# Half of an out-projection moved into the scan phase, and the chunks of the second phase staged anew

## The chip, the cores and the metric

The kernel runs on one core of one Trainium2 chip. The metric is the device time of one execution in microseconds (us); before the change its median is 3416.74 us over three runs (3415.76 to 3419.22). Lower is better.

## The reference, cut to what matters

Three layers of a decoder on x of shape (2, 2048, 512): a selective-scan mixer, cross attention over a context of 77 keys with 16 heads, and a feed-forward part with a sine in it. Each is followed by a residual sum and a layer norm.

```
xz = x @ W_in + b_in                      # 512 -> 2048, halves x_proj and z
u = silu(x_proj); B, C = split(u @ W_xproj + b_xproj)
dt = softplus(u @ W_dt + b_dt)
h[t] = h[t-1] * exp(dt * A) + dt * u * B  # 16 states for each of 1024 channels
y = (sum over states of h * C + D * u) * silu(z)
x = layernorm(x + y @ W_out + b_out)                                  # x1
x = layernorm(x + softmax(mask(q k^T / sqrt(32))) v @ wo + b_o)       # x2
hidden = x @ W1 + b1                                                  # 512 -> 2048
q = hidden + gain * sin(theta + 0.1 * hidden)
x = layernorm(x + relu(q) @ W2 + b2)
```

Both batches make 4096 tokens. Products with large weights are done with operands split in a high and a low float16 half, in three matmuls each (`split_product`, lines 40 to 42).

## The kernel before

**Phase one, the scan** (`selective_scan_phase`). Tokens are columns. There are 8 chunks of 512 tokens, and in each 64 "pairs" of two states for 128 channels. For each pair PE spreads dt and dt*u over the partitions (`rep_dt`, L295; `rep_dtu`, L306), ACT takes the exponential in PSUM (`exps`, L526), DVE multiplies by B (`dbu`, L642) and runs two scans (`scans`, L655), ACT saves the last column (`save_carry`, L532), POOL multiplies by C (`weigh`, L722), and PE sums over states (`sums`, L318). PE, ACT and POOL also produce the projections of the next chunk within the pairs of the running one, at places that class `Plan` gives by hand. In the last chunk nothing is left to produce after place 28; keys and values of the cross attention are made at places 40, 42, 44 and 46 (`KV_AT`). y goes to DRAM, transposed, 128 channels at a time (`store_y`).

**Phase two, attention and feed-forward** (`attention_ffn_phase`). All engines meet at the end of phase one, and then walk over 16 chunks of 256 tokens (two tiles of 128). The order on each engine is written out by hand in `front_back(c, ...)`: the front of chunk c (out-projection, x1, attention, x2) and the back of chunk b = c-1 (feed-forward) are interleaved. Body 0 has a front only, body 16 a back only; bodies 2 to 14 are loops. What matters here:

- PE computes `out_projection` of chunk c (48 matmuls of 512 columns) at the start of the body, into the two PSUM banks `sps`. Then come the transposes of x2 and x1, `hidden` 0 to 7 (two of 16 columns of w1 each, into two PSUM buffers `fps`), `second` 0 to 7 (w2, into `nat`), the queries' projection, `scores`, `probs_t` (transposes of the probabilities), `attend` (times v) and at the end `natural(... w_o ...)`, again into `sps`.
- ACT: `hid_out` (four evacuations), `sine`, `relu`, `exps`, `probs_out`, `values_high`; its tables for square root, sine and exponential change four times in a chunk.
- DVE: residuals, layer norm (`statistics`, `normalize`), `fraction` (two instructions, both operands in SBUF), `mix` (two), `act_low`, `masked`, `row_maximum`, `less_maximum`, `softmax_b`.
- POOL: bias adds of 128x1024 (L1524) and the low half of y (`y_low`, L1533).

The body 0 also splits w1 and w2 in high and low, piece by piece.

## Time and profile before

| what | us |
|---|---|
| profiled execution, its own time | 3416.91 |
| its span | 3415.2 |
| last scan chunk (64 pairs), first dbu to last scan | 1738.2 to 1966.3 |
| last store of y issued; first load of phase two issued | 1971.9; 1974.4 |
| body 0: queries' projection; first scores | 2009.6 to 2016.9; 2018.0 |
| last w_o matmul of chunk 0, and of chunk 15 (start of its residual on DVE, less 0.2) | 2062.4; 3351.2 |
| x2's bias add on POOL, first and last (15 chunks between) | 2071.3; 3357.3 |
| a chunk in the loop (2585.32 to 2670.66) | 85.34 |
| from the last w_o matmul to x2 normalized (2661.78 to 2665.82) | 4.0 |
| PE, three pairs with 24 projection matmuls, one `sums` and one skip product (1751.6 to 1760.8) | 9.2 |
| busy over the span: PE, DVE, ACT, POOL | 86%, 80%, 59%, 52% |
| a load of 1024 KB of y_t, of 512 KB of x, issue to landing (median) | 7.5, 8.1 |
| `y_low` 128x2048, `y` to high 128x2048 | 4.07, 1.91 |
| keys of one batch, values of one batch, on PE | 4.5 to 6.2, 4.1 |

Read it so: the chunks of phase two take 85.9 us each on average ((3351.2 - 2062.4) / 15), and they are 1289 of the 3415 us. In rows of the timeline the first number is the start, the second the time from the first start to the last end of the merged instructions or their sum; a matmul's record is longer than its share of PE, so a block's price is the distance between the starts of two blocks.

### The profile page before, as it was taken

What the parts mean: (1) busy time and instruction counts of PE and PEld (TensorE: products, weight loads), DVE (VectorE), ACT (ScalarE), POOL (GpSimd) and SP (SyncE); (2) the same over time, 40 slices, a digit from 0 to 9 for tenths busy, and PEclk for the clock granted to TensorE, in tenths of its full rate; (3) what the DMA queues carried; (4) which work ended last, traced back from release to release, by engine and by line L of the source; (5) the groups of instructions that cost most, each with busy time, mean ns of one, the idle gap of its engine ahead of it and who ended that gap; (6) DMA issues with size and microseconds to landing.
All of it is one profiled execution on the core that took longest, in us unless ns stands there. A gap on an engine that the chain in (4) does not pass through costs nothing. (4 is left out here: it accounts for less than half of the span.)

```text
span 3415.2 us, 49521 instructions
## 1 busy us (share of the span) xinstructions
PE 2934.8 (86%) x18996; PEld 1318.5 (39%) x18996; DVE 2738.8 (80%) x3098; ACT 1999.3 (59%) x3570; POOL 1777.3 (52%) x893
## 2 busy tenths in 40 slices
PE   5888879889889888798897849999999999999997
PEld 2222222222222222222221236666666666666664
DVE  3999999999999999999999966666666666666664
ACT  4776776677667667766775444444444444444444
POOL 3797988978888879889788611111111111111100
PEclk8999999999999999999997769999999999999999
DMA  4111111111111111111113140000000000000000
GB/s 144 50 47 59 48 55 41 47 59 47 35 59 53 47 61 47 54 41 47 59 41 112 34 150 8 26 26 25 25 25 25 26 26 25 25 25 25 25 7 13
DMA packets 92547, 153.66 MB, mean 45 GB/s; under 512 B 12002, under 2 KB 29026, under 8 KB 91875
## 3 DMA queue, kind: packets, MB, share of 16 engines
q1 hardware_dynamic: 92386, 151.54, 14.0%
q8 instruction: 99, 1.62, 0.2%
q14 instruction: 62, 0.50, 0.1%
HBM read 92.79 MB, written 58.72 MB: 44 GB/s over the span
## 5 line engine op out<-in xcount | busy, mean ns | idle before, releaser
L722 POOL TENSOR_TENSOR h<-h,c_rep 128x1024 f32<-128x1024 f32 x512 | 1198.3, 2355 | 309.4 <-ACT carry L532 308.7
L655 DVE TENSOR_TENSOR_SCAN h<-r_ps,carry,h 128x512 f32<-128x512 f32 x768 | 942.8, 1272 | 7.2 <-ACT r_ps L526 6.5
L526 ACT ACTIVATE r_ps<-r_ps,decay 128x512 f32<-128x512 f32 x1024 | 632.0, 656 | 334.0 <-PE r_ps L295 333.3
L642 DVE TENSOR_TENSOR h<-u_ps,b_rep 128x1024 f32<-128x1024 f32 x512 | 618.7, 1208 | 44.3 <-PE u_ps L306 43.5
L1524 POOL TENSOR_TENSOR x<-x,rows 128x1024 f32<-128x1024 f32 x32 | 76.4, 2388 | 975.8 <-PE tr L961 975.8
L306 PE MATMUL u_ps<-dtu,spread 32*128 32x512 f16 x2048 | 326.6, 398 | 110.5 <-DVE h L642 109.4
L295 PE MATMUL r_ps<-dt,spread 32*128 32x512 f16 x2048 | 324.5, 396 | 75.5 <-DVE h L655 62.7
L318 PE MATMUL y_ps<-h,gather 128*32 128x512 f32 x2048 | 297.6, 650 | 55.6 <-POOL h L722 55.6
L655 DVE TENSOR_TENSOR_SCAN h<-r_ps,zero,h 128x512 f32<-128x512 f32 x256 | 313.9, 1269 | 6.9 <-ACT r_ps L526 6.7
L40 PE MATMUL nat<-region,act 128*128 128x512 f16 x512 | 206.8, 404 | 94.5 <-DVE act L1378 48.4
L40 PE MATMUL fps<-x,region 128*128 128x256 f16 x1024 | 280.9, 274 | 3.8 <-issue 2.4
L41 PE MATMUL fps<-x,region 128*128 128x256 f16 x1024 | 280.5, 274 | 0.0
L42 PE MATMUL fps<-x,region 128*128 128x256 f16 x1024 | 280.4, 274 | 0.0
L295 PEld LDWEIGHTS r_ps<-dt,spread 32*128 32x128 f16 x2048 | 58.5, 93 | 430.0 <-DVE h L655 244.0
L1154 ACT ACTIVATE units<-fps,turns 128x256 f32<-128x256 f32 x256 | 106.9, 468 | 191.7 <-PE fps L42 190.9
L40 PE MATMUL pj<-x_high,region 128*128 128x512 f16 x484 | 191.8, 396 | 31.7 <-ACT zs L467 12.6
L532 ACT ACTIVATE carry<-h 128x2 f32<-128x2 f32 x512 | 103.1, 201 | 189.9 <-DVE h L655 188.4
L40 PE MATMUL pj<-u_high,region 128*128 128x512 f16 x512 | 204.5, 399 | 4.9 <-ACT soft L499 3.7
L41 PE MATMUL nat<-region,act 128*128 128x512 f16 x512 | 205.0, 400 | 0.0
L42 PE MATMUL nat<-region,act 128*128 128x512 f16 x512 | 204.8, 400 | 0.0
L41 PE MATMUL pj<-u_low,region 128*128 128x512 f16 x512 | 203.0, 397 | 0.0
L42 PE MATMUL pj<-u_high,region 128*128 128x512 f16 x512 | 202.9, 396 | 0.0
(222 smaller groups left out, 5653.8 us busy)
## 6 DMA issues: line engine op xcount, KB each, us to landing
u_t_dram<-u SPq DMA_DIRECT2D x16, 1024.0 KB, 4.9
z_t_dram<-zs SPq DMA_DIRECT2D x32, 512.0 KB, 3.0
uz<-u_t_dram SPq DMA_DIRECT2D x64, 256.0 KB, 3.8
uz<-z_t_dram SPq DMA_DIRECT2D x64, 256.0 KB, 4.2
y_t_dram<-y SPq DMA_DIRECT2D x64, 256.0 KB, 2.4
y_t<-y_t_dram SPq DMA_DIRECT2D x15, 1024.0 KB, 7.5
x_in<-dram_x SPq DMA_DIRECT2D x16, 512.0 KB, 8.1
result<-x SPq DMA_DIRECT2D x16, 512.0 KB, 3.4
```

Of the source, the lines that this page charges most:

```text
L40: nc.tensor.matmul(out, w[0], x[0], start=start, stop=False)
L41: nc.tensor.matmul(out, w[0], x[1], start=False, stop=False)
L42: return nc.tensor.matmul(out, w[1], x[0], start=False, stop=stop)
L295: last = nc.tensor.matmul(r_ps[:, 2 * (pair % 2) + o, :], spread[32 * i:32 * i + 32, p // 2, :], dt16[32 * i:32 * i + 32, s, j, :], start= ...
L306: last = nc.tensor.matmul(u_ps[:, o, :], spread[32 * i:32 * i + 32, p // 2, :], dtu16[32 * i:32 * i + 32, s, j, :], start=(s == 0), stop=( ...
L318: last = nc.tensor.matmul(y_ps[32 * i:32 * i + 32, :], gather[:, q, :], h[:, g % H_GROUPS, i, :], start=(q == 0), stop=(q == 3))
L526: nc.scalar.activation(bank, bank, ACT.Exp, scale=decay[:, col:col + 1]).then_inc(s_da, 1)
L532: nc.scalar.activation(carry[:, j * NSTATE + 2 * p:j * NSTATE + 2 * p + 2], h[:, pair // 2 % H_GROUPS, o:o + 2, TS - 1], ACT.Copy).then_in ...
L642: nc.vector.tensor_tensor(h[:, g % H_GROUPS, o:o + 2, :], u_ps[:, :, :], b_rep[:, c % 2:c % 2 + 1, :].broadcast_to([P, 2, TS]), ALU.mult). ...
L655: nc.vector.tensor_tensor_scan(row, r_ps[:, 2 * (pair % 2) + o, :], row, start, ALU.mult, ALU.add)\
L722: nc.gpsimd.tensor_tensor(rows, rows, c_rep[:, c % 2:c % 2 + 1, :].broadcast_to([P, 2, TS]), ALU.mult)\
L1154: nc.scalar.activation(arg[:, n % 3, i, :], fps[:, n % 2, i, :], ACT.Identity, bias=turns[:, f:f + 1], scale=UNSCALE * 0.1 / TWO_PI)
```

## The change

1. `out_projection` leaves the chunk. For chunks 0 to 7 (16 tiles of 128 tokens) it runs in the last scan chunk, at pairs 28 to 59, half a tile (12 matmuls) in each pair; w_out is split there at places 18 to 28, y tiles are read back from DRAM, and the product goes to a DRAM tensor `o`. For chunks 8 to 15 it runs in bodies 0 (three chunks), and 1 to 5 (one each), behind the queries' projection, a tile at a time; its result goes to `o` too.
2. Keys and values move from places 40, 42, 44, 46 to 60, 61, 62, 63.
3. x1 is x + o + b_out, added on POOL (two adds of 128x1024), in the body before; its layer norm is in the middle of the body before.
4. `second` 6 and 7 of a chunk move into the next body, in front of and behind x1's transposes; there are 18 bodies now, and the final layer norm is one body later. x1 and x2 have two buffers each. x1's transposes and the queries use `sps`, not `tr`.
5. Within a chunk `hidden` 0 and 1 stand in front of the queries' projection.
6. `scores` interleaves two lanes (two groups of 32 rows), where it took one lane after the other.
7. POOL's x2 bias add waits for half of the scores.

Phase one (the constants and the pieces on PE and POOL):

```
-KV_AT = (40, 42, 44, 46)
+KV_AT = (60, 61, 62, 63)
+OUT_TILES = 16
+W_OUT_AT, OUT_AT = 18, 28
...
+            def out_piece(i, part):
+                if part == 0:
+                    pe.wait_ge(s_oe, i) if i else pe.wait_ge(s_ev, NC * PIECES)
+                pe.wait_ge(s_yl, 2 * i + part + 1)
+                for k in range(4 * part, 4 * part + 4):
+                    tokens = slice(k % 4 * P, k % 4 * P + P)
+                    last = split_product(nc, pj[:, :], [y16[s][:, i % 4, part, tokens] for s in range(2)],
+                                         [w_out[s][:, k, :] for s in range(2)], k == 0, k == NJ - 1)
+                if part == 1:
+                    last.then_inc(s_op, 1)
...
+            def w_out_low(k):
+                pool.wait_ge(s_wos, k // 2 + 1)
+                nc.gpsimd.tensor_tensor(w_out[1][:, k, :], w_out_raw[:, k, :], w_out[0][:, k, :], ALU.subtract)\
+                    .then_inc(s_wol, 1)
+
+            def y_low(i, r):
+                g = i % 4
+                pool.wait_ge(s_yh, i + 1)
+                nc.gpsimd.tensor_tensor(y16[1][:, g, r, :], w_out_raw[:, 2 * g + r, :], y16[0][:, g, r, :], ALU.subtract)\
+                    .then_inc(s_yl, 1)
```

Phase two, the order on PE:

```
+    def body(c, par, batch, front, back, late, ops, more):
+        b, d = c - 1, c - 2
+        if late:
+            second(d, 6)
+        if front:
+            x1_transposed(c, par, back)
+        if late:
+            second(d, 7)
+        if back:
+            x2_transposed(c, par)
+        if back:
+            hidden(b, 0)
+            hidden(b, 1)
+        if front:
+            queries(c)
+        for m in ops:
+            out_projection(c, m, 0)
+            out_projection(c, m, 1)
+        if back:
+            hidden(b, 2)
+        if front:
+            scores(c, 0, batch, (0, 1), ops)
+        if front:
+            scores(c, 0, batch, (2, 3), ops)
         if back:
             hidden(b, 3)
             second(b, 0)
         if front:
+            scores(c, 1, batch, (0, 1), ops)
+        if back:
+            hidden(b, 4)
             second(b, 1)
         if front:
+            scores(c, 1, batch, (2, 3), ops)
+        if back:
+            hidden(b, 5)
             second(b, 2)
+            hidden(b, 6)
             second(b, 3)
+        if front:
+            probs_t(c, 0, (0, 1))
+        if back:
             hidden(b, 7)
         if front:
             probs_t(c, 0, (2, 3))
         if back:
+            second(b, 4, (0,))
         if front:
             attend(c, 0, batch)
             probs_t(c, 1, (0, 1))
         if back:
+            second(b, 4, (1,))
         if front:
             probs_t(c, 1, (2, 3))
         if back:
+            second(b, 5, (0,))
         if front:
             attend(c, 1, batch)
         if back:
+            second(b, 5, (1,))
+        if front:
+            attention_out(c)
```

The order on ACT, its later part:

```
+    def body(c, par, batch, front, back, late, ops, more):
...
+            relu(b, 2)
             sine(b, 3)
+            hid_out(b, 4)
             relu(b, 3)
             sine(b, 4)
+        if front and not back:
+            weights_high(6)
+        if front:
+            exps(c, 0)
+        if back:
             hid_out(b, 5)
             relu(b, 4)
         if front:
+            exps(c, 1)
+        if more:
+            deviation("x1", 0, c + 2)
+        if back:
+            sine(b, 5)
             hid_out(b, 6)
+            relu(b, 5)
             sine(b, 6)
+        if front and not back:
+            weights_high(7)
+        if front:
+            probs_out(c, 0, (0, 1))
+        if back:
             hid_out(b, 7)
+        if front:
+            probs_out(c, 0, (2, 3))
+        if back:
             relu(b, 6)
             sine(b, 7)
         if front:
             values_high(c, 0)
             probs_out(c, 1, (0, 1, 2, 3))
```

The order on DVE, from the first `fraction` on:

```
+    def body(c, par, batch, front, back, late, ops, more):
+        b, d = c - 1, c - 2
...
         if back:
             fraction(b, 0)
             fraction(b, 1)
             mix(b, 0)
+        if front:
+            masked(c, 0, (0, 1))
+            masked(c, 0, (2, 3))
+        if back:
             fraction(b, 2)
             act_low(b, 0)
+            mix(b, 1)
+        if front:
+            row_maximum(c, 0)
+            masked(c, 1, (0, 1))
+        if back:
+            act_low(b, 1)
+            fraction(b, 3)
+            mix(b, 2)
+        if front:
+            masked(c, 1, (2, 3))
+            less_maximum(c, 0)
+        if back:
+            act_low(b, 2)
+            mix(b, 3)
+        if front:
+            row_maximum(c, 1)
+        if back:
+            fraction(b, 4)
+            act_low(b, 3)
+        if front:
+            less_maximum(c, 1)
+        if back:
+            mix(b, 4)
+        if front:
+            probabilities(c, 0)
+        if back:
+            act_low(b, 4)
+            fraction(b, 5)
+        if more:
+            statistics("x1", 0, c + 1, x1[:, 1 - par, :, :])
+        if front:
+            probabilities(c, 1)
+        if more:
+            normalize("x1", 0, c + 1, x1[:, 1 - par, :, :])
+        if back:
+            mix(b, 5)
             fraction(b, 6)
+            act_low(b, 5)
             mix(b, 6)
             fraction(b, 7)
             act_low(b, 6)
...
```

The order on POOL:

```
+    def body(c, par, batch, front, back, late, ops, more):
+        for m in ops:
+            for t in range(NT):
+                y_low(m * NT + t, t)
+        if front:
+            x1_bias(c, par)
+        if back:
+            pool.wait_ge(s_scp, b_scores(c, front))
+            x2_bias(c - 1, 1 - par)
+        if more:
+            x1_sum(c + 1, 1 - par)
+    def b_scores(c, front):
+        return c * 8 + 4 if front else CHUNKS * 8
```

`softmax_b` is now named `probabilities`. `x1_sum` is two adds of 128x1024 (o and b_out, then x), `x1_bias` and `x2_bias` one each.

## Rows read from the trace of the kernel before

**Rows 1.** Windows of the last scan chunk: us, busy of each engine, granted clock, DMA.
```profile
1780.00:1820.00 40.00, 34.77 (x208) 10.01 (x207) 39.89 (x36) 29.06 (x55) 37.03 (x21) 0.99 0.11 34
1820.00:1860.00 40.00, 30.53 (x160) 5.66 (x160) 39.59 (x36) 20.49 (x43) 36.91 (x21) 0.71 0.53 186
```

**Rows 2.** Timeline of PE in one chunk: start, us, engine, line, operands, idle before.
```profile
2491.09 0.38 PE L40 MATMUL sps<-w_out,y 128*128 128x512 f16 x1
...
2498.86 1.04 PE L961 MATMUL tr<-ident,x 128*128 128x128 f32 x8
...
2502.53 0.28 PE L40 MATMUL fps<-x,region 128*128 128x256 f16 x1
...
2511.03 1.09 PE L961 MATMUL tr<-ident,x 128*128 128x128 f32 x8 [0.46 <-DVE x L1356]
...
2517.69 0.38 PE L40 MATMUL nat<-region,act 128*128 128x512 f16 x1 [2.95 <-issue]
...
2520.28 0.27 PE L40 MATMUL tr<-xa,w_q 128*128 128x256 f16 x1
...
2528.20 1.62 PE L992 MATMUL sps<-k_t,q_t 32*128 32x77 f32 x16
2529.76 0.28 PE L40 MATMUL fps<-x,region 128*128 128x256 f16 x1
```

**Rows 3.** Timeline of DVE in one chunk, from the last scores on.
```profile
2627.51 0.99 DVE L1394 TENSOR_TENSOR pr<-sps,cap 128x308 f32<-128x308 f32 x2 [2.09 <-PE sps L992]
2628.53 1.44 DVE L1400 TENSOR_REDUCE smax<-pr 128x16 f32<-128x1232 f32 x1
2629.89 0.42 DVE L1362 TENSOR_SCALAR units<-units 128x512 f32<-128x512 f32 x1
...
2630.94 0.68 DVE L1378 SCALAR_TENSOR_TENSOR act<-units,act 128x512 f16<-128x512 f32 x1
2631.55 1.44 DVE L1404 TENSOR_TENSOR pr<-pr,smax 128x1232 f32<-128x1232 f32 x1
2632.90 1.43 DVE L1411 TENSOR_REDUCE ssum<-pr 128x16 f32<-128x1232 f32 x1
...
2636.01 0.42 DVE L1362 TENSOR_SCALAR units<-units 128x512 f32<-128x512 f32 x1
...
2640.18 1.66 DVE L1373 SCALAR_TENSOR_TENSOR units<-units,gain 128x256 f32<-128x256 f32 x4
```

**Rows 4.** Timeline of ACT in the same chunk.
```profile
2633.33 0.84 ACT L1154 ACTIVATE units<-fps,turns 128x256 f32<-128x256 f32 x2 [2.23 <-PE fps L42]
...
2634.78 1.24 ACT L1174 ACTIVATE pr<-pr 128x1232 f32<-128x1232 f32 x1
2636.04 1.28 ACT L1164 ACT_TABLE_LOAD   x1
```

**Rows 5.** Timeline of body 0: POOL and DVE beside each other.
```profile
2003.21 2.99 POOL L1524 TENSOR_TENSOR x<-x,rows 128x1024 f32<-128x1024 f32 x1 [17.92 <-PE tr L961]
...
2003.92 4.44 DVE L1293 SCALAR_TENSOR_TENSOR region<-act,region 128x2048 f16<-128x2048 f32 x1
...
2021.65 4.36 POOL L1533 TENSOR_TENSOR y<-y_t,y 128x2048 f16<-128x2048 f32 x1 [15.45 <-ACT y L1127]
2022.02 4.09 DVE L1383 TENSOR_SCALAR cap<-mask_i 128x154 f32<-128x154 int32 x1
```

**Rows 6.** Source line L1383 on DVE: durations in ns, min/median/max.
```profile
L1383 DVE TENSOR_SCALAR cap<-mask_i x16: 233/235/4094, 2022.0 to 3302.4; 128x154 f32<-128x154 int32 x16
```

**Rows 7.** Timeline of PE in body 0, the first matmuls after an idle stretch.
```profile
2009.64 0.37 PE L40 MATMUL tr<-xa,w_q 128*128 128x256 f16 x1 [6.51 <-DVE xa L1299]
...
2010.23 0.42 PE L40 MATMUL tr<-xa,w_q 128*128 128x256 f16 x1
2010.44 0.42 PE L41 MATMUL tr<-xa,w_q 128*128 128x256 f16 x1
...
2013.99 0.27 PE L40 MATMUL tr<-xa,w_q 128*128 128x256 f16 x1
```

More of the change, by code:

```diff
@@ L981, in hidden, with second, scores @@
                     last.then_inc(s_hp, 1)
-            def scores(c, t, batch, lanes):
+            def second(b, n, tiles=range(NT)):
+                if n == 0:
+                    pe.wait_ge(s_wlo, W2_SPLIT)
+                    pe.wait_ge(s_rw2, b * NT)
+                pe.wait_ge(s_actl, b * NU + n + 1)
+                for t in tiles:
+                    last = natural(nat[:, t, :], act16, w_2, NF, t, 2 * n, 2 * n + 2)
+                    if n == NU - 1:
+                        last.then_inc(s_w2, 1)
+            def scores(c, t, batch, lanes, ops):
                 for lane in lanes:
@@ L1078, in front_back @@
                     hidden(b, 5)
-                if front:
-                    scores(c, 1, batch, (2, 3))
-                if back:
+                    second(b, 2)
+                    hidden(b, 6)
                     second(b, 3)
-                    hidden(b, 6)
-                    second(b, 4)
-                    hidden(b, 7)
                 if front:
@@ L1266, in front_back @@
                 if back:
-                    relu(b, 7)
-                if not back:
-                    weights_high(10)
+                    relu(b, 6)
+                    sine(b, 7)
                 if front:
@@ L1272, in front_back @@
                     probs_out(c, 1, (0, 1, 2, 3))
+                if back:
+                    relu(b, 7)
+                if front:
                     values_high(c, 1)
-                if not back:
-                    weights_high(11)
-                if back and not front:
-                    deviation("w2", 2, b)
-            all_chunks(act, front_back)
+                if front and not back:
+                    weights_high(8)
+                    weights_high(9)
+            all_chunks(act, body)
         @block.vector
@@ L1443, in front_back @@
-                    normalize("outproj", 0, c, x1)
-                if not back:
-                    weights_low(4)
-                    weights_low(5)
+                    mask(c)
+                if late:
+                    normalize("w2", 2, d, x2[:, par, :, :])
+                if front and not back:
+                    for n in range(2, 6):
+                        weights_low(n)
                 if back:
@@ L1478, in front_back @@
                 if front:
-                    masked(c, 1, (2, 3))
-                    row_maximum(c, 1)
+                    probabilities(c, 0)
                 if back:
+                    act_low(b, 4)
                     fraction(b, 5)
-                    act_low(b, 4)
+                if front and not back:
+                    weights_low(6)
+                if more:
+                    statistics("x1", 0, c + 1, x1[:, 1 - par, :, :])
                 if front:
-                    less_maximum(c, 1)
@@ L1509, in front_back @@
                 if back:
[L1510 to L1511 removed]
+                    act_low(b, 7)
+                if front and not back:
+                    weights_low(8)
+                    weights_low(9)
                 if front:
[L1513 to L1517 removed]
@@ L1519, in _ @@
-            all_chunks(dve, front_back)
+                    for t in range(NT):
+                        residual_wo(c, par, t)
+            all_chunks(dve, body)
         @block.gpsimd
         def _(pool):
-            def add_bias(x, row, done):
-                nc.gpsimd.tensor_tensor(x[:, :, :], x[:, :, :], rows[:, row:row + 1, :].broadcast_to([P, NT, D]), ALU.add)\
-                    .then_inc(done, 1)
-            def bias_x_in(c):
-                pool.wait_ge(s_xin, (c + 1) * 16)
-                add_bias(x_in, 0, s_xb["xin"])
@@ new lines, in _, with body @@
+            pool.wait_ge(s_rows, 3 * 16)
+            x1_sum(0, 0)
+            def body(c, par, batch, front, back, late, ops, more):
+                for m in ops:
+                    for t in range(NT):
+                        y_low(m * NT + t, t)
+                if front:
+                    x1_bias(c, par)
+                if back:
+                    pool.wait_ge(s_scp, b_scores(c, front))
+                    x2_bias(c - 1, 1 - par)
+                if more:
+                    x1_sum(c + 1, 1 - par)
```

685 lines of the change are left out of this document (368 added, 317 removed).

## The prediction, on record before the result

> **What bounds the kernel now.** I read the windows first, then PE's timeline over one chunk of phase two, then DVE, ACT and POOL beside it. In the last scan chunk DVE is busy for 39.9 of 40 us while PE has 34.8 and, once production is over, 30.5 at a clock of 0.71 [rows 1]: DVE sets the pace, at 228.3 / 64 = 3.57 us a pair (its back-to-back distance is 3.48), and POOL with 37 of 40 is close behind. In phase two PE sets it. A chunk of 85.3 us has few idle places on PE, such as the 2.95 us ahead of `second` 0 [rows 2]. Distances between starts price PE's blocks: a matmul of 512 columns 0.215 us (12 in 2.59), one of 256 columns 0.11, two lanes of scores 1.56, the out-projection 7.77 for its first 36 matmuls and 10.35 for all 48 [rows 2]. All blocks of a chunk sum to 75.9 us, 9.4 of 85.3 are idle.
>
> **The chunk without the out-projection.** PE's work falls to 65.5, and to about 62.4 if two lanes of scores take 0.8 instead of 1.56. That would be 23 us less a chunk, but only if PE is never kept waiting, so I walk through the new orders with the distances of rows 3 and 4: `fraction` 1.05, `mix` 0.8, `act_low` 0.6, `masked` of two lanes 0.95, `row_maximum` and `less_maximum` 1.35 each, `probabilities` 3.1 (2632.90 to 2636.01) [rows 3]; `hid_out` 1.45, exponential 1.25, table load 1.28, sine and relu 0.55 [rows 4]. Zero is the last w_o matmul of the chunk before.
> - x2 is normalized at 4.0, as now. PE meanwhile has `second` 6, x1's transposes, `second` 7 and reaches x2's transposes at 6.05; high half on ACT to 8.2, low half on DVE to 9.5, `hidden` 0 starts at 9.7 (2.8 us idle). `hidden` 1 ends at 14.9, the queries at 20.2, `hidden` 2 at 22.8.
> - Scores of lanes 0 and 1 to 23.6; `masked` to 24.8; lanes 2 and 3 to 25.7 (1.3 us idle, since they wait for both banks); `masked` to 26.8. `fraction` 2, `act_low` 0: done 28.5, just when `hidden` 3 ends on PE. Then `second` 0, scores, `hidden` 4, `second` 1, scores: 38.0.
> - From 38.2 DVE has no gap but 0.4: `masked` 0.95, `less_maximum`, `act_low` 2, `mix` 3, `row_maximum`, `fraction` 4, `act_low` 3, `less_maximum`, `mix` 4, `probabilities` 0, `act_low` 4, `fraction` 5, x1's statistics 1.6, `probabilities` 1, x1's normalize 1.1, `mix` 5, `fraction` 6: 22.3 us, to 60.5. ACT's `sine` 6 waits for that, and `probs_out` of the first quarters stands behind it in ACT's order. PE is through with `hidden` 7 at 54.2 and waits in `probs_t(c, 0, (2, 3))` until 61.1: 7 us, with `second` 4 and 5 queued behind.
> - Behind it 15.1 us of work (transposes 1.8, `second` 4 and 5 5.2, `attend` 2.0, w_o 5.2, and 0.9 for the second half of the quarters) and small waits: **77.0 us**.
>
> So even without disturbance 14 to 15 us of the 23 come back as waits: PE's list was shortened where it was not the only limit.
>
> **POOL in the chunk.** New is where POOL's adds stand. When DVE or POOL works with operands in SBUF, one is held by the other: `mask`'s instruction of 0.23 us took 4.09 beside `y_low` [rows 5, 6], and it ended with it. Of two DVE instructions in a row, the waiting POOL add came between (its record is 2.99 instead of 2.36, and the second DVE instruction 4.44 instead of 2.29) [rows 5]. Now POOL's x2 bias add is released by half of the scores, at 25.8, and two more adds (o with b_out, x with o) stand behind it at once: 7.1 us. `fraction` 2 at 26.8 is held to 28.2, its second instruction by the second add to 31.0, `act_low` 0 by the third to 34.0. `second` 0 starts at 34.7, not 28.6: +6.1, and everything behind it moves along. Bounds: 0, if the adds let DVE through, and 7.1.
>
> The Trainium skill ("SBUF — State Buffer", Who interferes with whom) says that a DVE instruction with two SBUF inputs, or in a two-port mode, and a GpSimd instruction exclude each other for a whole instruction, and that issue order decides. By issue order alone, with DVE's next instruction issued ahead of POOL's next add, `act_low` 0 would slip through earlier, the delay would be about 3, and the sum below some 45 us smaller; the alternation seen in this trace speaks for 6.1.
>
> **The clock.** After 6.5 us of idle PE ran at half speed (0.21 us a matmul of 256 columns, against 0.11) from 2009.6 to 2013.9 [rows 7]; that loses 2.1 us. The new chunk has two such gaps, 6.4 us ahead of `second` 0 and 7 us ahead of `probs_t`. I count the first fully, 2.1, and 0.4 for the second, whose slow matmuls run beside ACT's `hid_out` 7 and `probs_out`. Bounds: 0 and 5. A chunk: 77.0 + 6.1 + 2.5 = **85.6**, against 85.9 on average now.
>
> **Scores in pairs.** Two lanes are 1.56 us now, one behind the other [rows 2]; no row has them interleaved. `rep_dt` and `rep_dtu`, which do interleave groups of 32 rows, put four matmuls of 512 columns into 0.43 us. I take 0.8; the bounds are 0.4 and 1.6, so a chunk is at most 3 longer.
>
> The Trainium skill ("TensorEngine Tiling (Array Packing)", Key Properties) has tiles of 32 rows work in parallel in weight load and matmul, which gives the 0.8; by the row of the sequential lanes alone the sum would be 45 us larger.
>
> **Chunks with out-projection.** Bodies 1 to 5 have 48 more matmuls behind the queries: 5 x 10.35 = +51.7. y's halves are ready in time there (its loads have a whole body, POOL's two halves of 2.05 lie ahead of the place that hurts), and nothing behind them had slack to give back.
>
> **Body 0.** It has three chunks' worth. PE's part is 31.0 instead of 10.35, +20.7, and that is the lower bound. But `y_t` holds one tile now, so each tile goes load (5, an estimate between nothing for its half size and 8.1 for as many KB of x), high half 1.0, low half 2.05, about 8.6 with hand-overs, where its matmuls take 5.2. Queries end near 2007 in old times, 10 us earlier, since x1 no longer waits for a product; six tiles end near 2060; scores start there and not at 2018: +42. The 4.09 + 2.7 us that the mask lost go away, x1's norm of the next chunk and one more weight piece come in: +40 to +44. I take **+42**, bounds 21 and 55.
>
> **The scan's last chunk.** Out-projection puts 12 matmuls, 2.58 us, on PE in each of 32 pairs. Three pairs with 24 such matmuls took 9.2 us; less these and one skip product that leaves 0.66 a pair for the two spreads and 1.0 for `sums` of every second pair; with the skip product of every eighth, 2.58 + 0.66 + 0.5 + 0.13 = 3.87 a pair against DVE's 3.5: PE becomes the bound, 32 x 0.35 = +11. Its clock is full then. POOL gets 8 pieces of w_out of 1.15 in places 20 to 27, where it was at 37 of 40 us [rows 1]: +5, and half a tile of y in each later pair (2.36 + 1.15 = 3.5, just inside). Keys and values, 17 us on PE, lay beside DVE's work at places 40 to 46; at 60 to 63 only four pairs are left to hide them, and `sums` of the last pairs, the last store and the end of the phase wait behind them: +9. Sum **+25**, bounds 5 (all hidden but a few waits) and 45.
>
> **The end.** Bodies 16 and 17: `hidden` 0 starts 9.7 instead of 8.4 after the last w_o, but PE has run before it; the last `second`s and the norm are the same. 0.
>
> **The sum**: 25 + 42 + 51.7 + 15 x (85.6 - 85.9) = 114. From the profiled execution, 3416.9 (0.2 from the median of the runs), to **3530**. Solved for the chunk, the change pays only under 85.9 - 118.7 / 15 = 78.0 us.
>
> **The rivals.**
> 1. *The chunk really gets shorter (faster).* If POOL's adds do not get in between, the chunk is 77.0, or less where an engine starts earlier than I walked; with PE's 11 us in the scan and 25 in body 0 the sum is 11 + 25 + 51.7 - 133.5 = -46: 3371. It decides from 78.0 us a chunk down. For it: PE loses 13.5 us of work a chunk. Against it: the 7 us wait for DVE's list does not depend on POOL. Chance 0.26.
> 2. *POOL costs half.* A chunk of 80 and the rest as forecast: 118.7 - 88.5 = +30, 3447. The alternation speaks against it. 0.14.
> 3. *The clock goes down for longer.* PE's share of the chunk falls from 89% to 73%, and in the last scan chunk, where it is like that, the clock was 0.71 [rows 1]. Four gaps at 2.1 and the scores at 1.5: a chunk of about 91.5, sum 118.7 + 84 = +203: 3620. Against it: single gaps of 3 us left no trace in most chunks. 0.10.
>
> **How the numbers follow.** Forecast 0.50, its own range 3485 to 3585. The range 3370 to 3590 takes in the first two rivals but for half of the first, and leaves out the third. What can be told from no change is 0.2%, 7 us. Faster 0.25, same 0.02, slower 0.73: the sums of the cases with a point from each side for the middle.
>
> **What would show it.** Right: PE in a chunk of the loop idle in front of `nat` (`second` 0) for about 6 us with `act_low` 0 as releaser, and about 7 in front of `probs_t`; `fraction` and `act_low` with records of 2 to 3 us beside L1524's successors; chunks of 83 to 88; the last scan chunk near 250; the first w_o of body 0 some 65 us later than before. Wrong: no long DVE records, a chunk below 78; or a body 0 as long as before.

## The result, and the profile after

The changed kernel takes 3570.09 us (median of four runs, 3568.44 to 3570.57) where the kernel before, in runs beside it, took 3416.76. The ratio is 1.0447, with a 95% interval of 1.0429 to 1.0465: 4.5% slower. The prediction was 3530.

The profiled executions (spans 3415.2 and 3568.9) divide at three events that both have: SP's first load of phase two, the last residual of x2 in chunk 0, and the one in chunk 15.

| stage | before | after | difference | predicted |
|---|---|---|---|---|
| up to the first load of phase two | 1974.4 | 2003.7 | +29.3 | +25 |
| body 0, to its last x2 residual | 88.2 | 131.6 | +43.4 | +42 |
| 15 chunks, to the last x2 residual of chunk 15 | 1288.7 | 1374.3 | +85.6 | +47.2 |
| the end | 63.8 | 59.3 | -4.5 | 0 |

A chunk of the loop is 88.7 us ((3456.61 - 2658.52) / 9, from the start of x2's bias add on POOL), one with an out-projection 99.0 (2372.63 to 2471.63). The scan's last chunk and body 0 have the size of the forecast. The chunk of the loop is 3.1 us longer than the forecast's 85.6; over the fifteen chunks that makes 38.4 and not 46, since the last of them, with little behind it, takes only 80.6.

The windows of the last scan chunk, as [rows 1], and two more behind them (columns as there):
```profile
1780.00:1820.00 40.00, 35.48 (x212) 9.84 (x204) 39.03 (x35) 30.90 (x55) 36.05 (x21) 0.96 0.07 27
1820.00:1860.00 40.00, 26.51 (x136) 7.12 (x136) 28.75 (x26) 23.30 (x45) 38.92 (x27) 0.70 0.41 129
1860.00:1900.00 40.00, 40.00 (x252) 13.69 (x252) 36.06 (x32) 21.93 (x42) 36.47 (x24) 1.00 0.61 189
1900.00:1940.00 40.00, 40.00 (x256) 13.79 (x249) 37.36 (x34) 22.93 (x43) 36.05 (x21) 1.00 0.32 99
```
From 1820 to 1860 DVE is busy for 28.8 us where it had 39.6 [rows 1], and POOL is full with 38.9. From 1860 on PE is busy for all 40 us at a granted clock of 1.00, and DVE no longer is: PE is the bound now.

PE's timeline over one chunk of the loop, as [rows 2] (start, us, engine, line, operands, idle before). Zero of the prediction's walk is 3074.05 here.
```profile
3083.64 0.27 PE L40 MATMUL fps<-x,region 128*128 128x256 f16 x1 [2.50 <-issue]
...
3090.54 0.27 PE L40 MATMUL sps<-xa,w_q 128*128 128x256 f16 x1
...
3098.50 1.12 PE L1166 MATMUL sps<-k_t,q_t 32*128 32x77 f32 x16
...
3100.65 1.55 PE L1166 MATMUL sps<-k_t,q_t 32*128 32x77 f32 x16 [1.04 <-DVE pr L1542]
...
3110.58 0.38 PE L40 MATMUL nat<-region,act 128*128 128x512 f16 x1 [4.47 <-DVE act L1527]
...
3114.95 1.12 PE L1166 MATMUL sps<-k_t,q_t 32*128 32x77 f32 x16
...
3135.05 1.09 PE L1180 MATMUL sps<-ident,pr 128*77 128x128 f32 x8 [1.74 <-DVE pr L1562]
...
3145.52 1.96 PE L1180 MATMUL sps<-ident,pr 128*77 128x128 f32 x8 [6.76 <-ACT p_t L1347]
```
The walk had `hidden` 0 at 9.7 (here 9.6), `second` 0 at 34.7 (36.5), and 7 us of idle time ahead of the second `probs_t` (6.76). Of the 1.8 us by which `second` 0 is later, 1.7 are `hidden` 0 and 1, which take 6.90 us and not 5.24. In phase two the waits of the `probs_t` for ACT's `p_t` sum to 103.8 us, the largest sum that PE has there; those of the `second`s for `act_low` sum to 71.7.

DVE and POOL in the same chunk, from the second pair of scores on; these rows answer to [rows 3] and [rows 5]:
```profile
3102.22 0.86 DVE L1542 TENSOR_TENSOR pr<-sps,cap 128x308 f32<-128x308 f32 x2 [1.62 <-PE sps L1166]
3102.31 2.35 POOL L1709 TENSOR_TENSOR x<-x,rows 128x1024 f32<-128x1024 f32 x1 [21.99 <-PE sps L1166]
3103.01 1.94 DVE L1512 TENSOR_SCALAR units<-units 128x512 f32<-128x512 f32 x1
3104.61 2.53 POOL L1698 TENSOR_TENSOR o_in<-o_in,rows 128x1024 f32<-128x1024 f32 x1
3104.98 2.71 DVE L1515 TENSOR_TENSOR units<-units 128x512 f32<-128x512 f32 x1
3107.22 2.66 POOL L1701 TENSOR_TENSOR x<-x,o_in 128x1024 f32<-128x1024 f32 x1
3107.61 2.82 DVE L1527 SCALAR_TENSOR_TENSOR act<-units,act 128x512 f16<-128x512 f32 x1
3110.36 0.87 DVE L1522 SCALAR_TENSOR_TENSOR units<-units,gain 128x256 f32<-128x256 f32 x2
```
POOL's three adds and DVE's `fraction` 2 and `act_low` 0 take turns, one instruction each. Three DVE instructions of 0.42, 0.69 and 0.68 us have records of 1.94, 2.71 and 2.82, and `act_low` 0 ends where PE's wait ends.

ACT in that chunk, as [rows 4], ahead of the second wait:
```profile
3134.80 1.28 ACT L1281 ACT_TABLE_LOAD   x1
3138.22 0.30 ACT L1281 ACTIVATE std<-mv,eps 128x2 f32<-128x2 f32 x1 [2.13 <-DVE mv L1499]
3138.53 1.28 ACT L1330 ACT_TABLE_LOAD   x1
...
3143.20 0.63 ACT L1336 ACTIVATE act<-units 128x512 f16<-128x512 f32 x1 [1.29 <-DVE units L1522]
3144.27 0.63 ACT L1330 ACTIVATE units<-units 128x512 f32<-128x512 f32 x1 [0.43 <-DVE units L1515]
3144.80 1.06 ACT L1347 ACTIVATE p_t<-sps 77x512 f32<-77x512 f32 x2
```
`probs_out` (L1347) has had its input since 3135.98 and starts at 3144.80, behind x1's square root, `sine` 5, `hid_out` 6, `relu` 5 and `sine` 6 in ACT's list.

Body 0, out-projection on PE (answers to [rows 7]; each row opens one tile, the tile at 2048 opens without a wait):
```profile
2040.69 0.61 PE L40 MATMUL sps<-w_out,y 128*128 128x512 f16 x1 [4.07 <-POOL y L1713]
...
2060.85 0.61 PE L40 MATMUL sps<-w_out,y 128*128 128x512 f16 x1 [6.79 <-POOL y L1713]
...
2068.71 0.39 PE L40 MATMUL sps<-w_out,y 128*128 128x512 f16 x1 [1.21 <-POOL y L1713]
...
2080.86 0.61 PE L40 MATMUL sps<-w_out,y 128*128 128x512 f16 x1 [6.79 <-POOL y L1713]
...
2088.12 0.39 PE L40 MATMUL sps<-w_out,y 128*128 128x512 f16 x1 [0.37 <-POOL y L1713]
...
2094.25 1.12 PE L1166 MATMUL sps<-k_t,q_t 32*128 32x77 f32 x16 [0.78 <-ACT o_out L1313]
```
The six tiles take 53.6 us, to the first scores. The mask's first instruction, 4.09 us before, is short there now; the longest of its 16 records is 2.07 (answers to [rows 6]):
```profile
L1532 DVE TENSOR_SCALAR cap<-mask_i x16: 206/224/2066, 2029.5 to 3439.7; 128x154 f32<-128x154 int32 x16
```

### The profile page after: what moved, and what is told of

It reads as the page before. It is cut to its first block and busy times, and to the rows that moved or that the text cites. A ratio compares the mean times of both kernels' runs of the same rounds, so it can differ in the third digit from the quotient of the medians.

```text
span 3568.9 us, 48928 instructions
## 1 busy us (share of the span) xinstructions
PE 2930.3 (82%) x18996; PEld 1309.3 (37%) x18996; DVE 2764.7 (77%) x3063; ACT 2038.5 (57%) x3638; POOL 1842.7 (52%) x950
## 5 line engine op out<-in xcount | busy, mean ns | idle before, releaser
L345 PE MATMUL u_ps<-dtu,spread 32*128 32x512 f16 x2048 | 319.4, 390 | 103.3 <-DVE h L731 102.7
L334 PE MATMUL r_ps<-dt,spread 32*128 32x512 f16 x2048 | 315.7, 388 | 57.2 <-DVE h L744 44.7
L357 PE MATMUL y_ps<-h,gather 128*32 128x512 f32 x2048 | 287.6, 630 | 57.5 <-POOL h L811 57.5
L40 PE MATMUL fps<-x,region 128*128 128x256 f16 x1024 | 294.7, 288 | 39.6 <-issue 31.7
L41 PE MATMUL fps<-x,region 128*128 128x256 f16 x1024 | 294.4, 288 | 0.0
L42 PE MATMUL fps<-x,region 128*128 128x256 f16 x1024 | 294.0, 287 | 0.0
L40 PE MATMUL nat<-region,act 128*128 128x512 f16 x512 | 211.1, 412 | 71.7 <-DVE act L1527 71.7
L1713 POOL TENSOR_TENSOR y<-y_t,y 128x1024 f16<-128x1024 f32 x16 | 36.3, 2270 | 411.5 <-ACT y L1307 411.5
L40 PE MATMUL pj<-x_high,region 128*128 128x512 f16 x484 | 192.0, 397 | 31.8 <-ACT zs L519 12.7
L41 PE MATMUL nat<-region,act 128*128 128x512 f16 x512 | 210.6, 411 | 0.0
L42 PE MATMUL nat<-region,act 128*128 128x512 f16 x512 | 208.7, 408 | 0.0
L40 PE MATMUL pj<-u_high,region 128*128 128x512 f16 x512 | 204.6, 400 | 4.9 <-ACT soft L551 3.8
```

The lines of the kernel that those rows point to most:

```text
L40: nc.tensor.matmul(out, w[0], x[0], start=start, stop=False)
L41: nc.tensor.matmul(out, w[0], x[1], start=False, stop=False)
L42: return nc.tensor.matmul(out, w[1], x[0], start=False, stop=stop)
L334: last = nc.tensor.matmul(r_ps[:, 2 * (pair % 2) + o, :], spread[32 * i:32 * i + 32, p // 2, :], dt16[32 * i:32 * i + 32, s, j, :], start= ...
L345: last = nc.tensor.matmul(u_ps[:, o, :], spread[32 * i:32 * i + 32, p // 2, :], dtu16[32 * i:32 * i + 32, s, j, :], start=(s == 0), stop=( ...
L357: last = nc.tensor.matmul(y_ps[32 * i:32 * i + 32, :], gather[:, q, :], h[:, g % H_GROUPS, i, :], start=(q == 0), stop=(q == 3))
```

## The experiments

Twelve kernels. Ratios are against runs of the kernel before on the same chip (medians 3419 to 3422), so the changed kernel, at 1.0447, is to be read beside them. "Loop chunk" is the mean of nine, measured as above; "out chunk" is the mean of the last three or four with an out-projection.

| run | us | ratio, 95% interval | first load of phase two | loop chunk | out chunk |
|---|---|---|---|---|---|
| changed kernel | 3570.1 | 1.0447, 1.0429 to 1.0465 | 2003.7 | 88.7 | 99.0 |
| a1_adds_early | 3476.2 | 1.0163, 1.0146 to 1.0180 | 2001.5 | 82.3 | 92.2 |
| a2_queries_first | 3512.3 | 1.0274, 1.0256 to 1.0292 | 2002.5 | 85.3 | 94.8 |
| a3_filler | 3554.9 | 1.0403, 1.0385 to 1.0420 | 2002.7 | 86.9 | 99.2 |
| a4_tiny_low | 3563.5 | 1.0427, 1.0410 to 1.0445 | 1998.3 | 88.7 | 98.9 |
| a5_act_order | 3535.1 | 1.0333, 1.0307 to 1.0359 | 2001.7 | 85.3 | 99.0 |
| a6_three | 3392.1 | 0.9928, 0.9912 to 0.9945 | 2001.9 | 77.1 | 85.3 |
| a7_two_of_three | 3559.2 | 1.0409, 1.0391 to 1.0426 | 1994.7 | 88.7 | 99.0 |
| a8_kv_quarter | 3570.6 | 1.0441, 1.0424 to 1.0459 | 2003.4 | 88.7 | 99.0 |
| a9_two_y | 3557.8 | 1.0406, 1.0388 to 1.0423 | 2005.1 | 88.7 | 99.0 |
| a10_more_act | 3380.0 | 0.9888, 0.9871 to 0.9904 | 2002.8 | 75.5 | 85.1 |
| a11_best | 3366.1 | 0.9839, 0.9826 to 0.9853 | 2002.4 | 75.8 | 85.1 |
| b1_lanes | 3407.1 | 0.9964, 0.9953 to 0.9976 | 1974.9 | | |

**POOL's adds (a1_adds_early).**
```
                 if back:
-                    pool.wait_ge(s_scp, b_scores(c, front))
                     x2_bias(c - 1, 1 - par)
```


> Changed kernel (3570), but POOL's x2 bias add no longer waits for half of the scores; it is released by x2's transposes, with the two adds for the next x1 behind it. Theory (the adds hold DVE's fraction 2 and act_low 0, and with them PE's second 0): the three adds now lie beside hidden 0 and 1, where DVE has little to do; in a plain chunk the idle time ahead of second 0 falls from 5.8 us to about 0 or 1, the chunk from 88.5 to about 81 to 83, total 3450 to 3490. Rival (the hold is covered by the later wait ahead of probs_t, so moving it only moves the wait): the gap ahead of second 0 goes, the one ahead of probs_t grows from 6.8 to 12, total 3550 to 3575. Rival 2 (the adds do as much harm where they stand now, delaying x2's low half): total 3560 to 3600.

Measured: 3476.2, a loop chunk 6.4 us shorter and an out chunk 6.8. The theory holds, the rivals do not: the wait ahead of `probs_t` stayed at 6.76. The three adds now lie here, in a timeline of DVE and POOL:
```profile
2928.86 2.34 POOL L1709 TENSOR_TENSOR x<-x,rows 128x1024 f32<-128x1024 f32 x1 [1.12 <-PE tr L1096]
2929.95 1.23 DVE L1471 TENSOR_TENSOR x<-tr,x 128x1024 f16<-128x1024 f32 x1 [1.04 <-ACT x L1293]
...
2931.15 2.35 POOL L1698 TENSOR_TENSOR o_in<-o_in,rows 128x1024 f32<-128x1024 f32 x1
...
2933.58 2.35 POOL L1701 TENSOR_TENSOR x<-x,o_in 128x1024 f32<-128x1024 f32 x1
2933.64 2.39 DVE L1534 TENSOR_SCALAR cap<-cap 128x154 f32<-128x154 f32 x1
```
x2's low half, which reads PSUM (L1471), runs at its usual 1.23 beside the first add. The mask's second instruction is held from 0.24 to 2.39, where nobody waits for it. The same adds now stand beside work with slack. The gain has two parts: `second` 0 comes 4.7 us earlier, and it runs at full speed (2.69 us for 4.37).

**Part 5 undone (a2_queries_first).**
```
+                if front:
+                    queries(c)
                 if back:
                     hidden(b, 0)
                     hidden(b, 1)
-                if front:
-                    queries(c)
```
(and the same on ACT.)

> Changed kernel (3570) with part 5 undone: the queries' projection stands in front of hidden 0 and 1 again, on PE, and its evacuation in front of theirs on ACT. Theory A (queries fill the 2.5 us of idle time ahead of hidden 0 and hidden runs at full clock): -3 to -4 us a chunk, total 3510 to 3525. Theory B (what decides is DVE's list from masked on: scores come 5 us earlier but fraction 0 to 2 come 5 us later, so second 0 waits as before): total 3555 to 3590.

Measured: 3512.3, a loop chunk 3.4 us shorter, an out chunk 4.2. Theory A. In the changed kernel `hidden` 0 comes 2.5 us after x2's transposes, since it needs their low half; the queries need only x1's, which has been there, and fill that time. The block of `hidden` 0 and 1, 6.90 us in the chunk of the changed kernel shown above (3083.64 to 3090.54), runs at full clock here: `hidden` 0 to 2 take 7.96, 2.65 each. `second` 0 still waits 5.67 us for `act_low` 0, as theory B had it, but starts 32.5 us after `second` 6 and not 36.5.

**The clock (a3_filler).**
```
                     hidden(b, 3)
+                    for k in range(16):
+                        mm(tr[:, 0:2, :].rearrange(...), w_1[:, 0, 0, 0:P], w_1[:, 0, k % KD, 0:512], ...)
                     second(b, 0)
```


> Changed kernel (3570) with 16 more matmuls of 512 columns into a bank that nobody reads then, between hidden 3 and second 0: about 3.4 us of work, put into the 5.8 us in which PE waits for act_low 0. Theory (after this gap second 0 runs at half clock, 4.4 us for 2.6): second 0 takes 2.6 to 3.0, a chunk of the loop -1 to -2 us, total 3545 to 3560. Rival (the slow matmuls lie beside DVE's work, which sets the next step anyway): no change within 5 us. Rival 2 (the filler delays second 0): slower, 3575 or more.

Measured: 3554.9, 1.8 us less a loop chunk. `second` 0 in the changed kernel, and with the filler in front of it (PE's timeline, both):
```profile
3110.58 0.38 PE L40 MATMUL nat<-region,act 128*128 128x512 f16 x1 [4.47 <-DVE act L1527]
...
3111.45 0.63 PE L41 MATMUL nat<-region,act 128*128 128x512 f16 x1
3111.88 0.63 PE L42 MATMUL nat<-region,act 128*128 128x512 f16 x1
...
3114.44 0.58 PE L42 MATMUL nat<-region,act 128*128 128x512 f16 x1
```
```profile
3005.92 3.62 PE L1227 MATMUL tr<-region 128*128 128x512 f16 x16
3010.59 0.38 PE L40 MATMUL nat<-region,act 128*128 128x512 f16 x1 [1.05 <-DVE act L1530]
...
3011.45 0.38 PE L41 MATMUL nat<-region,act 128*128 128x512 f16 x1
...
3012.96 0.38 PE L42 MATMUL nat<-region,act 128*128 128x512 f16 x1
```
The distance of two matmuls is 0.43 us in the one (1.2 GHz) and 0.215 in the other (2.4 GHz); the block takes 4.37 and 2.68. So the work that is late pays the clock on top of the wait. The loop chunks alternate between 85.4 and 88.5 with the filler, and so do two prices. In the chunk shown `hidden` 0 and 1 took 6.91 us, PE waited 1.05 us behind the filler, and `second` 0 took 2.68. In the chunk before it `hidden` 0 and 1 took 5.23, PE reached the filler earlier and then waited 2.24 us, and `second` 0 had 4.37 again. What makes `hidden` 0 and 1 differ, behind the same gap of 2.5 us, stays open.

**The scan: POOL's pieces (a4_tiny_low), PE's matmuls (a7_two_of_three), keys and values (a8_kv_quarter).**
```
-  nc.gpsimd.tensor_tensor(w_out[1][:, k, :], w_out_raw[:, k, :], w_out[0][:, k, :], ALU.subtract)
+  nc.gpsimd.tensor_tensor(w_out[1][:, k, 0:8], w_out_raw[:, k, 0:8], w_out[0][:, k, 0:8], ALU.subtract)
```


> Changed kernel (3570), with the low half of w_out in the scan phase computed for 8 of 512 columns only; this leaves most of that subtraction out. It takes 8 x about 1.1 us from POOL in places 20 to 27 of the last scan chunk. Theory (POOL's backlog of these pieces delays DVE, 11 us of idle time there): first load of phase two 9 to 13 us earlier than in the changed kernel (2003.7), total 3557 to 3561. Rival (PE's 3.75 us a pair behind it would have been the bound anyway, the backlog is absorbed): 0 to 3 us, total 3567 to 3570.


```
-  last = split_product(nc, pj[:, :], [y16[s]... for s in range(2)], [w_out[s][:, k, :] for s in range(2)], ...)
+  nc.tensor.matmul(pj[:, :], y16[0]..., w_out[0][:, k, :], ...)
+  last = nc.tensor.matmul(pj[:, :], y16[1]..., w_out[0][:, k, :], ...)
```


> Changed kernel (3570) with two of the three float16 products in the out-projection of the scan phase; the product with w_out's low half is left out there: 8 matmuls a pair, not 12, 0.86 us less on PE in each of 32 pairs. Theory (PE, at 3.75 us a pair, is the bound in places 32 to 59, DVE would go on at 3.5 to 3.57): first load of phase two 6 to 9 us earlier, total 3561 to 3564. Rival (POOL with 3.5 us a pair is the bound there as well): 0 to 3 us.


```
-  for k in range(KD):
-      last = nc.tensor.matmul(pj..., wk[:, k, ...], ctx_t[:, k, b, :], ...)
+  last = nc.tensor.matmul(pj..., wk[:, 0, ...], ctx_t[:, 0, b, :], ...)
```
(keys; the values' loop takes one k likewise.)

> Changed kernel (3570) with a quarter of the products for keys and values (the sum over 128 of 512 rows; three quarters are left out): PE's 17 us at places 60 to 63 become 4 to 5. Theory (only four pairs are left to hide them, and the last sums and the last store wait behind them): first load of phase two 8 to 13 us earlier, total 3557 to 3562. Rival (what ends the phase is DVE's last scans and the gate, or the loads for keys and values): 0 to 3 us.

The start of the last scan chunk differs from run to run by some us with the same code ahead of it (1745.84 to 1752.37), so the three are compared by its length, from the store of y that ends the chunk before to the last store. In the changed kernel these are (SP's timeline):
```profile
1748.09 0.32 SPq L228 DMA_DIRECT2D y_t_dram<-y  x1
...
1836.35 0.32 SPq L228 DMA_DIRECT2D y_t_dram<-y  x1
...
1877.23 0.32 SPq L228 DMA_DIRECT2D y_t_dram<-y  x1
...
1970.24 0.32 SPq L228 DMA_DIRECT2D y_t_dram<-y  x1
...
2001.26 0.33 SPq L228 DMA_DIRECT2D y_t_dram<-y  x1
```
| length of the last scan chunk | us |
|---|---|
| before (1745.89 to 1971.93) | 226.0 |
| changed | 253.2 |
| a4_tiny_low | 249.4 |
| a7_two_of_three | 243.2 |
| a8_kv_quarter | 248.5 |

With a third of the out-projection's matmuls gone eight pairs take 28.45 us again, not 31.0: PE is the bound there, for 10 us in all. POOL's pieces of w_out are 3.8 us, keys and values 4.7 for three quarters of their products. a8_kv_quarter missed its expectation of 8 to 13: its first load of phase two is 0.4 us earlier and its total did not move. In the profiled execution its scan chunk began 4.3 us later, so the 4.7 are read from the stage alone, from one execution each. a4_tiny_low missed its expectation of 9 to 13 as well: most of the idle time there lies ahead of the first half tile of the out-projection, whose matmuls wait for POOL's `y_low` behind POOL's other work and then run at half clock. Most of that wait stayed, 3.49 us where the changed kernel has 5.38 (PE):
```profile
1851.51 0.59 PE L40 MATMUL pj<-region,u_high 128*128 128x512 f16 x1 [5.38 <-POOL u_low L837]
```
They stand in PE's order ahead of the next pair's spreads, and DVE waits 6.96 us for these, its longest wait while the pairs run (5.88 in a4_tiny_low).

**ACT's order (a5_act_order).**
```
+                if front and back:
+                    probs_out(c, 0, (0, 1))
                 if more:
                     deviation("x1", 0, c + 2)
                 if back:
                     sine(b, 5)
                     hid_out(b, 6)
+                if front and back:
+                    probs_out(c, 0, (2, 3))
                 if back:
                     relu(b, 5)
                     sine(b, 6)
```


> Changed kernel (3570) with another order on ACT alone: the evacuation of the first two quarters of the probabilities (probs_out) stands ahead of x1's square root and sine 5, and that of the last two behind hid_out 6, not behind sine 6. Theory (the 6.8 us of PE's idle time ahead of the second probs_t comes of ACT's list, where probs_out stands behind sine 6, and DVE's list behind that has slack): the gap falls to 0 or 1, a chunk of the loop from 88.5 to 82 to 84, total 3470 to 3500. Rival (DVE's list is the bound there: the wait moves to second 5, which needs act_low 5 behind mix 5): 1 to 3 us a chunk, total 3520 to 3555.

Measured: 3535.1, loop chunk -3.4, out chunk 0. The theory's expectation was missed; the total lies in the range of the rival, but PE does not wait at `second` 5 as the rival had it. The 6.76 us are gone, and 1.98 and 2.99 come back ahead of `attend` and the last `probs_t`, both of them waits for `p_t` in ACT's list. The other 1.7 are speed: `hidden` 0 and 1 take 5.24 us in nine of ten loop chunks where they took 6.90. In an out chunk it is the other way round, 6.90 for 5.24, and that gives the 1.8 us of saved waits back.

**The three together (a6_three)**, a1, a2 and a5 in one kernel.

> Changed kernel with three edits: POOL's x2 bias add not held until half of the scores, queries in front of hidden 0 and 1, and the ACT order of the run a5_act_order. Measured alone, the first two take 6.4 and 3.2 us off a chunk of the loop (88.5). Theory (the three gaps are separate places on PE's path): chunk 72 to 75, total 3570 - 94 - 58 - 70 to 90 = 3330 to 3350, faster than the kernel before (3417 to 3420). Rival (DVE's work of some 60 us a chunk becomes the bound between masked and mix 5): chunk 77 to 79, total 3395 to 3430.

Measured: 3392.1 and 77.1 a loop chunk. Singly the three took 94, 58 and 35 us, 187 in sum; together 178. So the three gaps are separate. The total was over its expectation because a5 had been expected to bring twice what it did. The chunk of 77.1 is in the range that the rival had, and the total is 3 us under it, but its reason, DVE as the bound, is not what the rows show: DVE is busy for 67% of the loop, and of PE's 7.5 us of waits in a chunk 4.0 are for ACT's `p_t` and 3.6 for DVE.

**What is left on ACT (a10_more_act).**
```
                 if more:
                     deviation("x1", 0, c + 2)
+                if front and back:
+                    probs_out(c, 0, (2, 3))
                 if back:
                     sine(b, 5)
                     hid_out(b, 6)
...
+                if front:
+                    values_high(c, 0)
+                    probs_out(c, 1, (0, 1))
                 if back:
                     hid_out(b, 7)
```


> The kernel a6_three (3392) with two more moves on ACT: probs_out of the last two quarters of tile 0 ahead of sine 5, and values_high 0 and probs_out of tile 1's first quarters ahead of hid_out 7. Theory (PE's idle times of 1.98 us ahead of the first attend and 2.98 us ahead of the last probs_t come of ACT's order): chunk from 76.9 to 72 or 73, total 3315 to 3335. Rival (hid_out 7 and sine 6 come late, so the wait moves to second 5 or to the next body's second 7): 0 to 1 us a chunk, total 3375 to 3395.

Measured: 3380.0, in the range of the rival, with 1.6 us less a loop chunk. In the timeline of a6_three PE had these waits; in a10_more_act the first is gone and the second became 2.41, but one of 0.7 to 2.3 us now stands ahead of the second `attend`:
```profile
2925.76 1.08 PE L1189 MATMUL tr<-p_t,v 77*32 77x128 f32 x32 [1.98 <-ACT p_t L1347]
...
2932.15 1.78 PE L1180 MATMUL sps<-ident,pr 128*77 128x128 f32 x8 [2.98 <-ACT p_t L1347]
```
So the waits only moved: they sum to 67.7 us over nine loop chunks of a6_three and to 71.7 in a10_more_act. What fell is the time at half speed, from 2.9 to 1.8 us a chunk (counted as in the next section), with a mean granted clock of 0.94 and 0.96. That is 1.1 of the 1.6 us; the expectation's reason, less idle time, is not what the rows show.

**Body 0 (a9_two_y).**
```
+        def y_place(i):
+            if i < OPS_FIRST * NT and i % 2:
+                return x2[:, 1, :, :]..., s_yt[1], i // 2 + 1
...
+                    for i in range(NT * len(ops)):
+                        out_evacuated(i, i % 2)
+                        if i + 2 < NT * len(ops):
+                            y_high(i + 2, i % 2)
```


> Changed kernel (3570) with a second buffer for y tiles in body 0 (x2's second half, free there), and on ACT each tile's high half directly behind the evacuation of the tile two before. Theory (body 0's six tiles take a chain of load, high half, low half and 4 to 7 us of idle time on PE for every second tile, 53 us in all from the first matmul, where PE's work is 6 x 5.2 = 31): the first scores of body 0 start 17 to 22 us earlier against the first out-projection, total 3548 to 3554. Rival (body 0 is held by DVE's splitting of w1 and w2 and their loads, so that the wait only moves): 0 to 8 us.

Measured: 3557.8. The six tiles take 39.7 us, not 53.6, from 2041.69 to the first scores at 2081.34. The mechanism is shown, the size was over-expected: one wait of 4.46 us remains, for a y tile whose load lands only at 2065.07.

**Lanes of scores in pairs, in the kernel before (b1_lanes).**
```
-                    for i in range(HU):
-                        last = mm(sps[:, unit % 2, ...], q_t[rows_of, i, ...], k_t[rows_of, batch, i, :], ...)
-                    last.then_inc(s_scp, 1)
+                for i in range(HU):
+                    for lane in lanes:
+                        last = mm(sps[:, lane % 2, ...], q_t[rows_of, i, ...], k_t[rows_of, batch, i, :], ...)
```


> The kernel before (3416.8) with part 6 alone: the scores of two lanes interleaved, 32 matmuls alternating between two groups of 32 rows. Theory (four pairs of lanes a chunk, 1.05 instead of 1.56 us each, all on PE's path): -2 us a chunk, total 3380 to 3395. Rival (scores lie ahead of waits for DVE, so PE gains nothing): total 3412 to 3417. If interleaving brought what I had taken for the forecast (0.8): 3370.

Measured: 3407.1, 0.36% under the kernel before, some 12 us and not 30. Two lanes take 1.05 us, not 1.56. A loop chunk is as long as before (85.3 against 85.4 us). In one chunk read block by block the 2.0 us saved are gone again: `second` 0, behind the same idle time as before, took 3.79 us for 2.59, the queries' projection behind it 5.71 for 5.24, and the wait ahead of `second` 4 grew from 3.13 to 3.51. `second` 0 took 3.79 us or more in 14 of 15 chunks here, 3.80 or more in 4 of 15 before. The two windows around that `second` 0, first of b1_lanes, then of before:
```profile
2599.00:2604.00 5.00, 4.28 (x15) 1.83 (x16) 4.94 (x10) 4.33 (x9) 0.00 (x0) 0.71 0.00 0
```
```profile
2602.00:2607.00 5.00, 3.96 (x25) 2.44 (x26) 4.94 (x9) 4.66 (x10) 0.00 (x0) 1.00 0.00 0
```
The clock in them is 0.71 and 1.00, with an idle time of 2.95 and 2.96 us ahead of the block.

**The best of these (a11_best)** is a10_more_act with body 0 of a9_two_y.

> The kernel a10_more_act (3380) with the y tiles and the ACT order of a9_two_y in body 0. Measured in the changed kernel, these took 13.9 us off body 0's out-projection (53.56 to 39.65). Theory (body 0 and the chunks are separate terms of the sum): 3364 to 3368, 1.6% under the kernel before. Rival (with a shorter body 0, DVE's splitting of w1 and w2 comes late for the first chunks): 3372 to 3380.

Measured: 3366.1, as the sum of the terms had it, and 1.6% faster than the kernel before. So the change as a whole pays once its orders are put right. How much of this is the moved out-projection is not shown: 0.4% is what the scores in pairs gave alone, and no run puts the new order of ACT into the kernel before.

## Why the prediction was right or wrong

The sign and the places of the waits were right, 40 of 153 us were missing, and 38 of these lie in the chunk. There the cost of the clock was put far too low, and part of the agreement in the other terms is luck.

- *The scan's last chunk, +25.* It is 27.1 us longer; the other 2.2 lay ahead of it and are run-to-run. PE as the bound, 3.87 us a pair: 31.00 / 8 = 3.875 measured, and a7_two_of_three takes 10.0 back where 11 were counted. Keys and values, +9: the last interval between stores grew from 22.7 to 31.0, +8.3, but that holds out-projection too: a7_two_of_three takes 2.0 off it and a8_kv_quarter 4.8, so about 6 are keys and values, an estimate. POOL's backlog, +5: the pieces of w_out are 3.8, but the two intervals to 1877.23 are 14.7 us longer, because the first half tile of y waits in the same backlog and then runs at half clock. That wait was not in the forecast. It was offset by a gain that was not in it either: in the places 40 and on, keys and values had cost the kernel before 3.4 us (its three intervals from 1860.52 to 1949.26 are 88.7 us, three of 28.45 are 85.3; that keys and values are the reason is read from their place, no run shows it). That the stage came out near +25 is in part luck. The forecast's 228.3 us for the last scan chunk is 228.1 by its own events; nothing hangs on it.
- *Body 0, +42:* +43.4. The chain of 8.6 us a tile was right on average (53.6 / 6 = 8.9), and a9_two_y shows that it is the chain and not PE.
- *Five out-projections, 10.35 each:* the block takes 10.36. The difference of the chunks, 99.0 - 88.7 = 10.3, hides two terms that cancel: in an out chunk `hidden` 0 and 1 take 5.24 us for 6.90, but 0.98 of idle time stand ahead of the block and 5.64, not 4.47, ahead of `second` 0. In a6_three the difference is 8.2.
- *The chunk without disturbance, 77.0:* the gaps stand where the walk put them, and a6_three, without the hold and with shorter gaps at `hidden` 0 and at the second `probs_t`, comes to 77.1. The two numbers are not the same sum, and their agreement is luck: the walk had 14.6 us of idle time in a chunk (77.0 - 62.4), a6_three has 7.5 by its records and pays 2.9 of clock, which the walk did not. One part of the walk was added up wrongly: the steps listed from 38.2 on sum to 21.7 us with the gap of 0.4, not 22.3.
- *POOL's hold, +6.1:* a1_adds_early gives 6.4 a loop chunk, and in one of these chunks `second` 0 starts 31.8 us after `second` 6, where it was 36.5 (-4.7), and takes 2.69, not 4.37 (-1.7). So the hold itself was smaller than forecast, and the clock behind it was part of its price. Alternation, instruction by instruction, is what the rows show. The Trainium skill ("SBUF — State Buffer", Who interferes with whom) states an exclusive lock, and the trace agrees (0.69 us became 2.71 beside adds of 2.53 and 2.66). By issue order alone, its other statement, the forecast had estimated a delay of about 3, and a1_adds_early shows 4.7.
- *The clock, +2.5:* this is the step that failed in size. Counting in PE's timeline the matmuls of `hidden` and `second` that start at about twice the full-speed distance from the one before them, a loop chunk of the changed kernel loses 5.5 us, 2.9 in `hidden` and 2.6 in `second`. The kernel before loses 1.9, nearly all in `second`. The transposes behind the 6.76 us wait take 1.76 for 0.88. The forecast counted `second` 0 fully (1.8 to 2.6 measured) and nothing for `hidden` 0 and 1, which in nine of ten loop chunks took 6.6 to 6.9 us for 5.24, behind a gap of only 2.5. "Single gaps of 3 us left no trace in most chunks" holds for `second` 0 of the kernel before, 2.59 us behind 2.96 in 11 of 15 chunks. It does not hold for its `second` 4, which took 3.99 to 4.28 us in all 15, for the same 12 matmuls (kernel before, PE):
```profile
2603.04 0.38 PE L40 MATMUL nat<-region,act 128*128 128x512 f16 x1 [2.96 <-issue]
...
2642.51 0.61 PE L40 MATMUL nat<-region,act 128*128 128x512 f16 x1 [3.13 <-DVE act L1378]
```
- *Scores, 0.8 for two lanes:* 1.05. Four pairs make 1.0 us a chunk.
- *The account of the chunk:* clock +3.9 (5.5 and 0.9 against 2.5), scores +1.0, hold -1.4 (4.7 against 6.1) are +3.5 where +3.1 was measured. The other small differences between the walk and the chunk are not taken apart.
- *Tail, 0:* -4.5; not taken apart.

Of the rivals, the third had the right direction, a clock that costs more. It had 91.5 us a chunk, and 88.7 lies midway between that and the forecast's 85.6; its sum is four gaps at 2.1 only, and the scores that it names would add 2.8 more. The second rival was refuted by the alternating records. The break-even of 78.0 us a chunk is bracketed, not met: at 77.1 and 85.3 the kernel is 0.7% faster than before, at 82.3 and 92.2 it is 1.6% slower.

## What to carry to other kernels

Where a bound engine is given less work, walk through the other engines' lists first: here some 12 us of PE's work left a chunk of the loop (10.35 and four times 0.5), and it became 3.3 us longer. Three edits of the order, one on POOL, one on PE and ACT, one on ACT, took 11.6 us off again. POOL's adds cost nothing here where DVE was reading PSUM or doing work that nobody waits for, and 6.4 us a chunk where it was not; ask what DVE will be doing when POOL's semaphore opens. Price each new gap on PE twice, as a wait and as slower matmuls behind it, and read that price from all chunks of a trace: one chunk of the kernel before showed `second` 0 without it, and `second` 4 of the same chunk with it.

## What the runs showed of the hardware that was not expected

- A gap of about 2.5 to 3 us ahead of a block cost nothing in one chunk and 1.2 to 1.7 us in another, with the same code: `second` 0 in the kernel before took 2.59 us in 11 chunks and 3.80 to 4.28 in four, always behind 2.95 or 2.96. In b1_lanes it took 3.79 or more in 14 of 15. There the saved matmul time came back as clock; in a10_more_act the gain came as clock while the waits stayed.
- Sixteen matmuls that nobody needs, put into a wait, made the kernel 15 us faster (a3_filler: 3554.9 for 3570.1).
- Interleaving two groups of 32 rows in float32 matmuls of 77 columns brought 1.05 us from 1.56 for 16 of them, a third and not a half.
- A DVE instruction of 0.24 us can stand for 2.39 behind a POOL add, while one that reads PSUM passes at 1.23 beside the same kind of add.
